# Attention's first stretch in a one-core macaron block: query rows loaded per half after four tiles, keys stored in six rows, first maxima between halves of products

## The reference

```python
x = x + 0.5 * ffn(layernorm(x))          # mixture of 16 experts, top 2, plus a shared expert
x = x + attn(layernorm(x), Wqkv, Wo)     # 32 heads of 16, ONE key and value head for all
x = x + 0.5 * ffn(layernorm(x))          # the same weights again
# x: (4, 256, 512): 4 batches of 256 tokens
def attn(h, Wqkv, Wo):
    qkv = h @ Wqkv                        # 512 -> 512 (q) + 16 (k) + 16 (v)
    scores = q . k * 16**-0.5 + slope[head] * (pos_k - pos_q), causal
    return softmax(scores) @ v @ Wo
```

## Time and profile before

| | |
|---|---|
| median of 3 runs | 521.96 us (518.97 to 521.98) |
| the profiled execution | 522.08 us; its span 520.3 us, mean granted clock 0.955 |
| busy share of the span | PE 85%, PEld 51%, DVE 50%, POOL 32%, ACT 29% |
| HBM | 47.66 MB read, 19.72 MB written |

### The profile page before, as it was taken

One profiled execution on the slowest core, in us unless ns is written; L12 is line 12 of the kernel. 1 busy time (PEld: TensorE's weight loads), 2 busy tenths in 40 slices (PEclk: granted clock), 3 DMA queues, 4 the chain that ended last, 5 costly groups with the idle time before them and its releaser, 6 DMA issues.

```text
span 520.3 us, 7969 instructions
## 1 busy us (share of the span) xinstructions
PE 444.8 (85%) x2540; PEld 265.3 (51%) x2541; DVE 258.0 (50%) x723; ACT 153.4 (29%) x316; POOL 166.8 (32%) x234
## 2 busy tenths in 40 slices
PE   1899779999979928679999899898979969999990
PEld 1534356666537626445665465345444446666630
DVE  5466602222268624557886686634346812222327
ACT  1411013223112201124664364465222113323210
POOL 2801125556304622222332232242001024556310
PEclk9999979999998969897999999999999979999996
DMA  8999923433286374522222100010120023433277
GB/s 242 316 326 326 280 63 130 142 104 138 106 312 224 67 191 96 109 67 84 71 66 70 50 17 4 3 64 24 38 82 0 2 82 101 142 119 123 101 255 289
DMA packets 49029, 65.40 MB, mean 126 GB/s; under 512 B 6948, under 2 KB 28348, under 8 KB 48954
## 3 DMA queue, kind: packets, MB, share of 16 engines
q1 hardware_dynamic: 40469, 42.52, 26.3%
q0 software_dynamic: 6528, 19.72, 11.7%
q10 hardware_dynamic: 2000, 2.76, 1.9%
HBM read 47.66 MB, written 19.72 MB: 130 GB/s over the span
## 4 chain that ended last, share of the span: by engine, by line
PE 64%; DVE 13%; issue 11%; DMA 5%; ACT 3%; SPq 2%; ACTq 0%; POOL 0%; POOLq 0%; DVEq 0%
PE ps L1383 15%; PE ps L1396 6%; PE ps L1241 6%; PE ps L1551 6%; PE ps L1523 4%; PE ps L1466 4%; PE ps L1369 4%; PE ps L1495 3%; DVE arena L1089 3%; DVE x L958 2%; PE ps L1292 2%; PE ps L1497 2%; PE ps L1509 2%; PE ps L1381 2%; PE ps L1533 2%
## 5 line engine op out<-in xcount | busy, mean ns | idle before, releaser
L1383 PE MATMUL ps<-w,arena 128*128 x304 | 79.2, 405 | 0.0
L1089 DVE TENSOR_REDUCE arena<-ps 128x3 f32<-128x384 f32 x128 | 66.6, 550 | 7.7 <-PE ps L1497 6.2
L589 POOL TENSOR_SCALAR_AFFINE_SELECT arena<-arena 128x512 f32<-128x512 f32 x64 | 40.9, 640 | 85.4 <-ACT arena L729 85.0
L729 ACT ACTIVATE arena<-ps 128x768 f32<-128x768 f32 x64 | 51.8, 812 | 53.2 <-PE ps L1511 52.4
L1383 PEld LDWEIGHTS ps<-w,arena 128*128 128x128 f32 x304 | 56.8, 197 | 11.4 <-issue 0.4
L519 POOL DMA_INDIRECT arena<-xn_dram,arena x40 | 39.1, 977 | 71.6 <-issue 46.3
L1241 PE MATMUL ps<-turns,arena 128*128 128x512 f32 x128 | 59.6, 596 | 0.0
L524 POOL DMA_INDIRECT y_dram<-arena x38 | 38.4, 1012 | 48.9 <-DVE arena L999 33.7
L1495 PE MATMUL ps<-cb 128*128 128x256 bf16 x128 | 37.0, 289 | 18.6 <-DMA arena<-q_dram 9.1
L993 DVE TENSOR_TENSOR arena<-ps,arena 128x128 f32<-128x128 f32 x38 | 11.1, 292 | 83.4 <-ACT arena L655 42.1
L999 DVE COPY arena<-ps 128x512 f32<-128x512 f32 x36 | 24.9, 692 | 31.9 <-PE ps L1396 26.5
(11 more groups left out here) (188 smaller groups left out, 639.7 us busy)
## 6 DMA issues: line engine op xcount, KB each, us to landing
arena<-y_dram SPq DMA_DIRECT2D x16, 512.0 KB, 7.5
arena<-q_dram SPq DMA_DIRECT2D x36, 128.0 KB, 2.8
xn_dram<-arena SPq DMA_DIRECT2D x16, 256.0 KB, 3.6
w<-in_L_ffn_ew_dram SPq DMA_DIRECT2D x4, 1024.0 KB, 10.0
q_dram<-arena SPq DMA_DIRECT2D x16, 192.0 KB, 2.8
x<-_attn_hidden_states_dram SPq DMA_DIRECT2D x4, 512.0 KB, 6.0
out_dram<-x SPq DMA_DIRECT2D x8, 256.0 KB, 3.6
turns<-in_L_ffn_sw_dram ACTq DMA_DIRECT2D x3, 512.0 KB, 6.8
```

The costliest lines, as they stand in the source:

```text
L589: pool.affine_select(diagonal, diagonal, [[0, 2], [0, 2], [1, P]], ALU.is_ge, 0.0, base=0, channel_multiplier=-1).then_inc(sem("sel"), 1)
L729: act.activation(pr[:, n % 2, pair, :], ps[:, bank:bank + 2, :].rearrange("p a b -> p (a b)")[:, 0:768], ACT.Exp).then_inc(sem("exp"), 1)
L1089: dve.tensor_reduce(m3[:, h:h + 1, :], ps[:, bank, 0:3 * P].rearrange("p (n k) -> p n k", n=3), AX_X, ALU.max).then_inc(sem("s_max"), 1)
L1383: ins = pe.matmul(o, xgT[:, par, c, :], w12[:, ds(e, 1), c, :], start=False, stop=(c == KC - 1))
```

## The change

Five things are changed, all between the first feed-forward part and the attention's main loop.

1. SP and POOL wait for `comb >= 4` in place of 8 before they write the first half of `qside` and `kT`; `hv` gets a tensor of its own, so that it isn't overwritten while tiles 4 to 7 are still to be combined. What goes into the second half of `qside` still waits for all eight. DVE does some of the `pairs_x` of tiles 5 to 7 later, behind `rest` of other items, and POOL issues its two DMAs ahead of the parts of batch 0.
2. SP's list: blocks 0 and 1 and the keys are stored, then heads 0 to 15 are loaded, then the keys; blocks 2 and 3 follow, and blocks 0 and 1 of batch 1 before heads 16 to 31 are loaded.
3. The keys are stored in six rows by three DMAs (`K_RUNS`: three parts, two, one) and loaded by one DMA of 96 partitions.
4. In batches 2 and 3 each product is cut in two halves of two instructions. One head stands between the halves and two behind the second (two and two for the last two items; `FIRST_COUNTS`). DVE takes the maxima of the early head and of the first late one before `rest`, the others after it.
5. The first turned maxima go to another bank (`m_bank`), so that the key product of batch 3 doesn't wait for `m_parts`; the main loop waits for it in its place.

```diff
-        k_dram = nc.dram_tensor("k_dram", (BATCH, 3, HD, SEQ), BF16).ap()
+        k_dram = nc.dram_tensor("k_dram", (BATCH, HD, len(KPART), SEQ), BF16).ap()
...
+        hv = sb("hv", [P, NT, CHOICES])
...
-        hv = view("ffn", [P, NT, CHOICES])
...
-        FIRST_HEADS = ((2, 0, 0), (2, 1, 3), (2, 2, 6), (2, 3, 8), (2, 4, 11), (3, 0, 14), (3, 1, 16), (3, 2, 19), (3, 3, 22), (3, 4, 25))
...
+        K_RUNS = ((0, 3), (3, 2), (5, 1))
+        FIRST_COUNTS = ((1, 2),) * 8 + ((2, 2),) * 2
+
+        def first_heads(b, n):
+            i = len(ITEMS) * (b - 2) + n
+            at = sum(c for counts in FIRST_COUNTS[:i] for c in counts)
+            half = at + FIRST_COUNTS[i][0]
+            return range(at, half), range(half, half + FIRST_COUNTS[i][1])
...
+        def m_bank(b, half):
+            return PS_S if (b, half) == (0, 0) else PS_A
...
-            for r in range(len(KPART)):
-                eng.dma_start(kT[r:R_REST:SPREAD, b], k_dram[b, KPART[r]]).then_inc(sem(f"q_in{b % 2}0"), 16)
+            eng.dma_start(kT[0:R_REST, b], k_dram[b].rearrange("d r t -> (d r) t")).then_inc(sem(f"q_in{b % 2}0"), 16)
...
-                        sp.dma_start(k_dram[b].rearrange("k d t -> d k t"), kp[:]).then_inc(sem("k_out"), 16)
+                        for at, count in K_RUNS:
+                            sp.dma_start(k_dram[b, :, at:at + count], kp[:, 0:count]).then_inc(sem("k_out"), 16)
...
-                if first == 0:
-                    sp.wait_ge(sem("k_out"), 16 * (b + 1))
-                    k_rows(sp, b)
                 for r in range(len(QPART)):
                     sp.dma_start(qside[r:R_REST:SPREAD, p, first:last],
...
+                if first == 0:
+                    sp.wait_ge(sem("k_out"), 16 * len(K_RUNS) * (b + 1))
+                    k_rows(sp, b)
...
-            outs(0)
-            sp.wait_ge(sem("comb"), NT)
+            outs(0, (0, 1, 2))
+            sp.wait_ge(sem("comb"), NT // 2)
             q_rows(0, 0, HEADS // 2)
+            outs(0, (3, 4))
             outs(1, (0, 1))
             q_rows(0, HEADS // 2, HEADS)
             outs(1, (2, 3, 4))
+            sp.wait_ge(sem("comb"), NT)
             q_rows(1, 0, HEADS)
...
-            for n in range(len(ITEMS)):
+            pool.wait_ge(sem("comb"), NT // 2)
+            pool.dma_start(qside[R_REST:R_MAX, 0], rows_q).then_inc(sem("rows_in"), 16)
+            pool.dma_start(kT[R_REST:ROWS], rows_k).then_inc(sem("rows_in"), 16)
+            for n in range(4):
                 parts(0, n)
-            pool.wait_ge(sem("comb"), NT)
-            pool.dma_start(kT[R_REST:ROWS], rows_k).then_inc(sem("rows_in"), 16)
-            pool.dma_start(qside[R_REST:R_MAX, 0], rows_q).then_inc(sem("rows_in"), 16)
             att_rstd(2)
-            for n in range(3):
+            parts(0, 4)
+            for n in range(2):
                 parts(1, n)
             att_rstd(3)
+            parts(1, 2)
+            pool.wait_ge(sem("comb"), NT)
...
+            for b in (2, 3):
+                for n in range(len(ITEMS)):
+                    early_heads, late_heads = first_heads(b, n)
+                    if (b, n) == (3, 2):
+                        maxima_parts(0, 0)
+                    for h in early_heads:
+                        maxima(0, h, PS_S + 1 + h % 2)
+                    maxima(0, late_heads[0], PS_S + 1 + late_heads[0] % 2)
+                    rest(b, n)
+                    for h in late_heads[1:]:
+                        maxima(0, h, PS_S + 1 + h % 2)
...
-                if b == 3:
-                    pe.wait_ge(sem("m_parts"), 1)
...
-                    if c is None:
-                        kv_product(b)
+                    product = (lambda chunks: kv_product(b, chunks)) if c is None else (lambda chunks: q_product(b, c, chunks))
+                    if b < 2:
+                        product(range(KC))
                     else:
-                        q_product(b, c)
...
+                        early_heads, late_heads = first_heads(b, n)
+                        product((0, 1))
+                        first_scores(early_heads)
+                        product((2, 3))
+                        first_scores(late_heads)
```

More of the change, by code:

```diff
@@ L1105, in maxima_parts @@
                     dve.wait_ge(sem("m_out"), 32 * n)
-                src = ps[0:QT * HEADS, PS_A, 0:P]
+                src = ps[0:QT * HEADS, m_bank(b, half), 0:P]
                 link(dve.tensor_copy(mp[:, 0, :], src))
@@ L1142, in att_dve @@
             att_stats(1)
-            rest(0, 0)
             link(dve.memset(vv[:], 0.0))
@@ L1146, in att_dve @@
             link(dve.memset(vv[:, :, :, HD:HD + 1], 1.0))
+            rest(0, 0)
             pairs_x(4)
@@ L1149, in att_dve @@
             rest(0, 1)
+            rest(0, 2)
             pairs_x(5)
-            rest(0, 2)
-            pairs_x(6)
             rest(0, 3)
-            pairs_x(7)
             values(0)
@@ L1157, in att_dve @@
             rest(0, 4)
+            pairs_x(6)
             att_norm(2)
             rest(1, 0)
+            pairs_x(7)
             rest(1, 1)
@@ L1166, in att_dve @@
             rest(1, 4)
-            def first_maxima(first, last):
-                for h in range(first, last):
-                    maxima(0, h, PS_S + 1 + h % 2)
-            for b, n, first in FIRST_HEADS:
-                if (b, n) == (3, 2):
-                    maxima_parts(0, 0)
-                rest(b, n)
-                first_maxima(first, first_until(b, n))
-                if n == 3:
-                    values(b)
-                if (b, n) == (3, 0):
-                    maxima_signed(0, 0)
+            for b in (2, 3):
[9 more added lines that the diff above has]
+                        maxima(0, h, PS_S + 1 + h % 2)
+                    if n == 3:
+                        values(b)
+                    if (b, n) == (3, 0):
+                        maxima_signed(0, 0)
             maxima_signed(0, 1)
@@ L1552, in out_product, with first_scores @@
                 ins.then_inc(sem("a_wo"), 1)
-            def first_scores(first, last):
-                for h in range(first, last):
+            def first_scores(heads):
+                for h in heads:
                     if h == 0:
@@ L1595, in att_pe @@
                         pe.wait_ge(sem("wo_in"), 16)
+                    if (b, q) == (0, 0):
+                        pe.wait_ge(sem("m_parts"), 1)
                     if more:
```

36 lines of the change are left out of this document (16 added, 20 removed).

## The result

| | before | changed |
|---|---|---|
| median | 521.35 us (518.97 to 521.98, 4 runs) | 504.13 us (500.1 to 506.5, 4 runs) |
| the profiled execution | 522.08 us, span 520.3 | 500.1 us, span 498.3 |
| mean granted clock | 0.955 | 0.970 |

The ratio is 0.967, with a 95% interval of 0.9594 to 0.9746: 17.2 us less by the medians, 22.0 us by the two traces. Of these 22.0 us, 1.7 lie ahead of the attention's first product (156.45 us before, 154.73 here). They are scatter: in the changed kernel's other two traces it starts at 156.73 and 156.41. The forecast was 499.3 us, 22.8 less. Two later series of the same kernel gave ratios of 0.9641 and 0.9608; the experiments come to why the series differ. Medians and ranges here are of all runs of a series, while the ratios leave out the few runs that took over 1.5% longer than the fastest of their kernel.

The account below looks back on a forecast made before the run. PE lost time to a hole, a slow clock behind it and small waits. 179.6 + 25.9 + 2.65 + 2.4 = 210.55 us ends the last score; main loop at 212.6, not 235.45: 22.8 less, 499.3 us, range 494 to 508.

Parts of the forecast that it names:

- The hole: PE idle 9.06 us before batch 2's first score; that score moves from 190.82 to 180.5 us, some 10.5 us.
- both doors: Two chains end the idle: query loads behind key loads on SP, and batch 1's store that ACT awaits; both must open earlier.
- The items: Product halves with heads in batches 2 and 3: eight of 2.54 us, two of 2.81, sum 25.9 us.
- The added waits: Waits added to the stretch: two early heads 0.6, maxima_parts 0.8, ACT's store at batch 3 1.0; together 2.4 us.
- The wait for the store: ACT at batch 3's block 0 waits for batch 2's first store, behind batch 1's loads: 1.0 us, bounds 0 and 3.
- signs of being wrong: ACT waiting for `q_dram` at batch 3's items, PE waiting for DVE between a product's halves, or a growing main loop.
- `maxima_parts`: DVE work of 1.1 us at batch 3's third item makes two maxima late: 0.8 us, bounds 0 and 1.7.
- The tail: From the last score's start at 210.3 us to the turn of the second maxima: 2.3 us, before 1.70.
- "better" rival: None of the 2.4 us of waits show and the clock stays up near the main loop's start: 494 to 496 us, chance 0.08.
- The handoffs: Rival: each of the ten items exposes 0.6 us more through semaphores and DVE's order: 505.3 us, chance 0.20.
- The loads weren't late: Rival denied here: query loads or ACT's block 0 still come near 190 us: about 510 us, chance 0.05.
- The clock didn't fall: Rival denied here: products cut by heads in two other banks run at the lower clock: 523.6 to 529 us, chance 0.07.

Follow-up runs that it names:

- Experiment 2: Changed kernel with the old items, old bank and key product's wait put back, leaving the change's parts 1 to 3 (loads) alone: 508.89 us, ratio 0.9782.
- Experiment 5: The kernel before, run again unchanged for a second trace: 521.39 us, one execution.
- experiment 6: Changed kernel without part 3: keys stored in three rows by one DMA and loaded by six behind the query loads: 507.79 us, ratio 0.9733.
- experiment 7: Changed kernel without part 1: SP and POOL wait for all eight tiles before the first loads: 509.42 us, ratio 0.9746.
- experiment 4: Changed kernel with the stores of batch 2's blocks 0 and 1 moved ahead of the loads of batch 1's 32 heads: 499.74 us, ratio 0.9609.
- experiment 11: The changed kernel, unchanged, a third time: 501.41 us against 521.74 for the kernel before, ratio 0.9608.
- experiment 8: Parts 1 to 3 with whole products and heads behind them, but DVE takes two maxima ahead of `rest`: 507.34 us, ratio 0.9715.
- experiment 9: On top of experiment 4, batch 1's keys are also stored ahead of the loads of heads 16 to 31: 499.0 us, ratio 0.9539.
- Experiment 10: On top of experiment 9, heads spread 4, 4, 4, then six times 3, then 2: 498.77 us, ratio 0.9554.

## Why the prediction held, and where it was off

**The hole.** Right, both doors. The first score was forecast at 180.5 with the product at 179.6, 0.87 apart; it is 0.97. Experiment 2 prices the loads in the first half at 11.5 us, where I had 10.5 for the hole and 1.7 for the cold product behind it. Experiment 5 speaks for two doors: in one execution whose query loads landed some 4 us earlier by themselves, the gain was 0.7 us. No run opened one door alone.

**SP's list.** The query loads were issued at 167.2 us, forecast 169.8; with the start 2 us earlier that is right to 1 us. Part 3, to which my sum gave no term of its own, is worth some 4 us (experiment 6), and the stores are where it shows: not the loads' lateness but what stands behind them. I had given batch 1's stores 3 us of room and said nothing of batch 0's blocks 2 and 3, which now stand behind the first loads. ACT waits for one of these in the changed kernel already (the line below), without a cost to PE. With these stores issued at 176.76 us (experiment 6) or 179.44 (experiment 7) in place of 171.82 the wait reaches PE.

```profile
174.07 0.37 ACT L714 CAST arena<-ps 128x256 bf16<-128x256 f32 x1 [1.45 <-DMA q_dram<-arena]
```

**The items.** Forecast 2.54 us and 2.81, measured 2.66 for the first and 2.91 for a key item. The key item is a mis-sized term: I had priced its product like the others', but its two halves start 0.98 us ahead of their heads, not 0.87, and two small gaps come on top: 0.7 us for the two key items of the stretch. The first half of the stretch is 15.53 us; by my terms (five items of 2.54, turns of 0.3, 0.5 and 1.35) 14.9.

**The added waits.** The wait for the store was put at 1.0 us with bounds of 0 and 3; PE lost 2.1 us (1.22 and 0.87), shown by experiment 4, and 2.7 in experiment 11. ACT waiting for `q_dram` at batch 3's items was one of my signs of being wrong, and it came: 4.68 us. So did an idle PE of over 1 us. `maxima_parts` was put at 0.8; PE doesn't wait for it at all. The two cancel to 0.3. The tail of 2.3 us from the last score was 2.56 (209.95 to 212.51). Together the stretch is 1.9 us longer than forecast: 0.6 in its first half, 1.3 in its second.

**Outside the stretch.** I expected 0.2 us less ahead of batch 2: from batch 0's key product to batch 2's first it is 17.8 us against 18.0. Behind the stretch nothing was to change: 285.25 to 285.79 against 284.85 and 285.45. But here two effects of the clock cancel. The windows run from the turn of the second maxima to DVE's first RECIPROCAL (the first heads weighed), and over the main loop's end; first before, then changed:

```profile
235.45:244.68 9.23, 9.21 (x63) 5.80 (x64) 6.43 (x14) 4.31 (x6) 2.57 (x4) 0.66 0.38 119
330.45:340.45 10.00, 7.57 (x89) 3.56 (x81) 6.64 (x20) 6.86 (x12) 5.13 (x8) 1.00 0.03 7
```

```profile
212.51:220.06 7.55, 6.76 (x63) 4.22 (x64) 6.26 (x14) 4.31 (x6) 2.57 (x4) 1.00 0.40 123
307.51:317.51 10.00, 7.35 (x69) 3.42 (x68) 4.60 (x17) 5.79 (x11) 4.59 (x7) 0.83 0.08 25
```

The clock that stays up at the loop's start is worth 1.7 us between these two traces (7.55 in place of 9.23; the others have 8.28 before and 8.29 and 7.55 changed), so my "better" rival had that part right. The 1.7 are still there at the RECIPROCAL of 309.19 us (333.81 before). At the one of 315.12 (338.47 before) 0.4 are left, for the clock falls there (0.83), where it hadn't fallen before. Behind the loop 1.4 more are lost, and the lower clock lasts longer there too (190 to 195 us behind the turn it is 0.56, against 0.94 before). In experiment 8, where the clock stays up at both of the windows above, the part behind is 283.14 us, 1.7 shorter than before. Why the falls come where they do stays open.

**The sum.** By the traces, 55.3 us of stretch became 35.1 (means of two and three): 20.3, and with 0.2 gained ahead of it and 0.4 given back behind it 20.1. The 0.4 is less than the parts behind differ among these kernels (283.14 to 287.58). Forecast 22.8. The medians of the three series say 17.2, 18.6 and 20.3. The first series was the smallest, and with it the target of the prediction, 504.13, lies in my range but 4.8 us above the forecast: 2.7 are there in the traces as well, the rest is scatter of executions whose traces I don't have. Where that lies stays open. That the first trace, 500.1 us, comes so near the 499.3 is in part luck, for 1.7 us of its gain lie ahead of the attention.

**The rivals.** The handoffs didn't show (0.1 us an item). The loads weren't late. The clock didn't fall: with products cut by heads in two other banks it was granted at 1.00 in every window from 180 to 212.5 us, and it had been 0.53 behind the hole. But my ground against this rival, that the clock had fallen behind idle PE, was only half right. The kernel before has a second fall, with no wait over 0.90 us since 198 us ahead of it:

```profile
210.57 3.37 PE L1466 MATMUL ps<-arena,turns 128*128 128x256 f32 x8 [0.75 <-ACT arena L687]
```

In its second trace the fall came at the key product (217.37 us), behind waits of 0.95 and 1.71. Experiment 2, with the same waits of 0.90, kept a clock of 1.00 from 180 to 222 us. The Trainium skill (TensorE: Matmul & The Clock Gate, "A second HAM failure mode: psum-queue depth-cycling") tells of a kernel of bf16 matmuls with 512 columns whose clock swung because PE paused often and briefly between groups of matmuls. The changed kernel's stretch doesn't show that, but it is no hard test either, since PE was busy for 8.00 us in the window of 180 to 188; the falls at 210.57 and 217.37 are of that kind, and experiment 2 speaks against it. Behind long waits the clock did fall: behind the 7.06 us of experiment 7 (a half product of 2.07 us at 187.33) and the 2.84 of experiment 6.

Part 5 was not tried by itself; that its wait is gone rests on experiments 2 and 8 (1.71 and 1.93 us) against the changed kernel.

## What to carry to other kernels

A queue that issues both stores and loads is a list of promises: before moving a load forward, ask which store now stands behind it and who waits for the buffer that this store frees. Here that wait turned up ahead of batch 2, at batch 3's first block and at the keys, and moved on each time one was mended. When a pipeline has a hole, look for every chain that ends at its far side; one of the two here could open 4 us earlier and gain 0.7. And on an in-order engine a short operation whose input is ready early should stand ahead of one that waits for a third engine: this alone gave 4.0 us, where cutting the products, the other bank and the new spread of the heads gave 3.7 together.

The best kernel of this study is experiment 9's, two moves in SP's list on top of the change: 499.0 us against 501.41 for the changed kernel in the same series, ratios 0.9539 (0.9503 to 0.9576) and 0.9608 (0.9574 to 0.9642). The intervals just touch; the stretch is 2 us shorter in the trace. Experiment 10 (498.77 us, 0.9554) can't be told from it.

## What the hardware showed unexpectedly

Two stores of 192 KB that SP issued from 170.91 us on in the kernel before, with no load in front, landed in 2.1 us (median of the two). With six loads of 128 KB ahead a store took 6.40, with six of 256 KB and the keys' load 6.21 (the changed kernel).

Six DMAs of 16 partitions cost SP 3.77 to 6.28 us of issue time, the same bytes in one DMA of 96 partitions 0.60.

The lower clock comes in pieces that shift between executions of one kernel (a product of 3.37 us at 210.57 in one trace of the kernel before, a key product of 3.47 us at 217.37 in the other), while the length of the stretch differed by 0.7 us. At the attention's start the same two products took 3.69 us in two of the thirteen traces (experiments 4 and 6), 5.17 to 5.38 in eight and 6.64 to 6.68 in three (experiments 7, 8 and 10); whoever compares single traces must look there first.
